# Operand stacks of a causal attention, built in another layout and filled through a scratch in memory

## The reference

```python
q = (x @ Wq.T).reshape(N, L, H, D).transpose(0, 2, 1, 3)     # H = 16 heads, D = 16
k = (x @ Wk.T).reshape(N, L, H, D).transpose(0, 2, 1, 3)
q = _layernorm(q, gq, bq)                                     # per head
k = _layernorm(k, gk, bk)
scores = jnp.einsum('nhld,nhmd->nhlm', q, k)
scores = jnp.where(causal, scores, NEG)
attn = jax.nn.softmax(scores, axis=-1)
```

## Time and profile before

| | us |
|---|---|
| median of 3 runs | 3621.69 (3620.69 to 3624.71) |
| the profiled execution | 3617.72 |
| its span, first to last instruction | 3615.8 |
| TensorE busy (matmuls) | 3336.7, 92% |
| VectorE busy | 2755.9, 76% |
| ScalarE busy | 2407.7, 67% |
| GpSimd busy | 1098.6, 30% |
| DMA queue of SP | 23.68 MB, 2.3% of 16 engines |

### The profile page before, as it was taken

How to read it: one execution, slowest core, us unless ns; L and a number is a source line. 1 busy time by engine, 2 the same in 40 slices (tenths; PEclk the granted TensorE clock), 3 DMA queues, 4 the chain that set the end, 5 groups by cost and what they waited for, 6 DMA issues and landing times.

```text
span 3615.8 us, 82601 instructions
## 1 busy us (share of the span) xinstructions
PE 3336.7 (92%) x31672; PEld 2617.6 (72%) x31672; DVE 2755.9 (76%) x5952; ACT 2407.7 (67%) x6425; POOL 1098.6 (30%) x778
## 2 busy tenths in 40 slices
PE   5999999999999999998999999999999999999998
PEld 4676776767777677776777767777676776767776
DVE  6877778777777877768777787787877878777775
ACT  6667676666766667666676666766667676666764
POOL 4351242412324223242222423124241242412320
PEclk8999999999999999999999999999999999999999
DMA  3000000000000000000000000000000000000000
GB/s 83 8 1 13 2 7 7 1 13 2 7 7 1 13 2 7 8 1 13 2 7 7 7 7 1 8 7 7 7 1 13 2 7 8 1 13 2 7 1 7
DMA packets 33863, 28.95 MB, mean 8 GB/s; under 512 B 8960, under 2 KB 33408, under 8 KB 33472
## 3 DMA queue, kind: packets, MB, share of 16 engines
q1 hardware_dynamic: 33472, 23.68, 2.3%
HBM read 15.28 MB, written 8.39 MB: 7 GB/s over the span
## 4 chain that ended last, share of the span: by engine, by line
PE 71%; ACT 14%; DVE 10%; issue 4%; POOL 1%; SPq 0%; DMA 0%; ACTq 0%; POOLq 0%; DVEq 0%
PE bank L696 14%; PE scores L810 11%; PE bank L707 9%; ACT prob L996 7%; PE scores L683 5%; PE bank L834 5%; PE scores L684 4%; PE scores L761 4%; PE scores L784 3%; PE bank L643 3%; PE scores L685 3%; PE bank L667 2%; DVE negmax L1265 2%; ACT qkt L937 2%; PE scores L679 2%
## 5 line engine op out<-in xcount | busy, mean ns | idle before, releaser
L996 ACT ACTIVATE prob<-scores,negmax 128x128 f32<-128x128 f32 (+3 forms) x2048 | 1059.3, 536 | 185.9 <-DVE negmax L1265 180.3
L1265 DVE TENSOR_REDUCE negmax<-scores 128x1 f32<-128x128 f32 (+3 forms) x2048 | 872.9, 482 | 54.8 <-PE scores L685 40.6
L696 PE MATMUL bank<-ident,prob 128*128 128x128 f32 x5120 | 725.8, 279 | 50.5 <-DVE probt L1273 43.4
L1273 DVE COPY probt<-bank 128x512 f32<-128x512 f32 x896 | 596.3, 683 | 171.5 <-PE bank L696 165.7
L696 PEld LDWEIGHTS bank<-ident,prob 128*128 128x128 f32 x5120 | 544.3, 141 | 163.7 <-issue 66.5
L685 PE MATMUL scores<-mask,ident 128*128 128x128 bf16 x2048 | 438.7, 226 | 0.0
L996 ACT ACTIVATION_READ_ACCUMULATOR prob<-scores,negmax 128x1 f32 x2048 | 434.8, 212 | 0.0
L683 PE MATMUL scores<-khh,qt 128*128 128x256 f32 (+2 forms) x1024 | 416.2, 407 | 13.3 <-POOL kll L572 13.3
L508 POOL TENSOR_TENSOR otl<-onm,oth 128x512 fp32r<-128x512 f32 x96 | 122.7, 1278 | 882.5 <-ACT oth L937 882.5
L521 POOL TENSOR_TENSOR rq<-ssq,expo 128x32 f32<-128x32 f32 x64 | 359.8, 5633 | 47.1 <-DVE ssq L1236 47.1
L503 POOL COPY rexp<-rsum 128x512 f32<-128x512 f32 x128 | 78.3, 611 | 964.8 <-DVE rsum L1277 964.8
(11 more groups left out here) (189 smaller groups left out, 6626.9 us busy)
## 6 DMA issues: line engine op xcount, KB each, us to landing
x_in<-in_x_rows SPq DMA_DIRECT2D x16, 512.0 KB, 3.8
out_rows<-x SPq DMA_DIRECT2D x16, 512.0 KB, 3.0
r_d<-in_wd SPq DMA_DIRECT2D x1, 1024.0 KB, 7.2
r_gu<-in_wg SPq DMA_DIRECT2D x2, 512.0 KB, 4.6
r_gu<-in_wu SPq DMA_DIRECT2D x2, 512.0 KB, 5.5
r_wob<-in_wo SPq DMA_DIRECT2D x4, 128.0 KB, 6.1
r_wqt<-in_wq_nope_t SPq DMA_DIRECT2D x1, 512.0 KB, 7.0
r_wqr<-in_wq SPq DMA_DIRECT2D x2, 256.0 KB, 8.5
```

Of the source, the lines that this page charges most:

```text
L696: ins = nc.tensor.transpose(bank[4 + n % 2][:, q * P:(q + 1) * P], prob[:, u % 2, q, i * P:(i + 1) * P], ident[:, :])
L996: nc.scalar.activation(prob[:, u % 2, q, 0:n], bank[q][:, 0:n], ACT.Exp, bias=negmax[:, a, u, q:q + 1], accum_out=sums[:, a, u, q:q + 1]). ...
L1265: nc.vector.tensor_reduce(negmax[:, a, u, M * part:M * part + M], scores[:, M * part:M * part + M, 0:n], axis=AX.X, op=ALU.max, negate=Tru ...
L1273: nc.vector.tensor_copy(probt[:, u % 2, i], bank[4 + n % 2][:, :]).then_inc(probt_dve.sem, 1)
```

## The change

The normalised queries and keys of a tile (512 channels, still fp32) are transposed first, in four fp32 transposes (`turn_qk`). Now channels are on partitions, in four blocks c, and tokens in rows. The split is made there: ScalarE copies the high part from PSUM and, later, the middle part (`high_part_qk`, `mid_part_qk`); VectorE makes the rest and the low part (`rest_qk`, `low_part_qk`). `part` holds the three parts of all four tiles. SP then stores each part to `stash` in memory (L459 of the new file) and loads it back into its slots of `qkt` (L466): a high part goes to three slots of the queries and three of the keys, a middle part to two and two, a low part to one and one. This is done for two halves, tokens 0 to 255 and 256 to 511: three stores and twelve loads each. A store has 128 partitions by 4 blocks by 256 tokens, a load 16 partitions (the channels of a head) by 16 heads by 256 tokens, so its rows have 512 bytes on both sides. Unit 0's scores wait for the first half's loads, unit 2's for the second half's; the first transposes of probabilities wait for all stores. The tables of steps are new.

```diff
-    res1 = at("res1", [P, 2 * C], F32, o + 10240)
-    stk = at("stk", [P, 2, 2 * H, SLOTS, D], BF16, o + 12288)
+    part = at("part", [P, 3, 4, L], BF16, o + 12288)
+    rest = at("rest", [P, 2, 4, P], F32, o + 24576)
...
+    stash = nc.dram_tensor("stash", (3, 4 * P, L), BF16, kind="Internal").ap()
...
-    QUADS_AT = {4: (0, 1, 2), 5: (3, 4, 5), 6: (6, 7), 7: (8, 9, 10), 8: (11, 12, 13), 9: (14, 15)}
-    CAST_AT = {2: 0, 3: 1, 5: 2, 6: 3}
-    REST_AT = {3: 0, 4: 1, 6: 2, 7: 3}
+    TURN_AT = {2: 0, 3: 1, 5: 2}
+    TURN_FIRST = {6: 3}
+    HIGH_AT = {3: (0,), 4: (1,), 6: (2, 3)}
+    MID_AT = {4: (0,), 5: (1,), 7: (2, 3)}
+    QUERY_SLOTS = ((0, 1, 2), (3, 4), (5,))
+    KEY_SLOTS = ((0, 3, 5), (1, 4), (2,))
...
+        def store_part(k, half, signal):
+            tokens = slice(half * 2 * P, (half + 1) * 2 * P)
+            sp.dma_start(stash[k].rearrange("(c p) l -> p c l", p=P)[:, :, tokens], part[:, k, :, tokens]).then_inc(signal.sem, 16)
+
+        def load_slots(k, half):
+            tokens = slice(half * 2 * P, (half + 1) * 2 * P)
+            for first, slots in ((0, QUERY_SLOTS[k]), (H, KEY_SLOTS[k])):
+                rows = stash[k][first * D:(first + H) * D].rearrange("(h d) l -> d h l", d=D)
+                for s in slots:
+                    sp.dma_start(qkt[s * D:(s + 1) * D, first:first + H, tokens], rows[:, :, tokens]).then_inc(stack_loaded[half].sem, 16)
+
+        def stack_rows(b, half):
+            if b > 0:
+                sp.wait_ge(stack_loaded[half].sem, stack_loaded[half].at(b, 0))
+            sp.wait_ge(high_ready.sem, high_ready.at(b, 2 * half + 2))
+            store_part(0, half, high_stored)
+            sp.wait_ge(mid_ready.sem, mid_ready.at(b, 2 * half + 2))
+            store_part(1, half, mid_stored)
+            sp.wait_ge(high_stored.sem, high_stored.at(b, 16 * (half + 1)))
+            load_slots(0, half)
+            sp.wait_ge(low_ready.sem, low_ready.at(b, 2 * half + 2))
+            store_part(2, half, low_stored)
+            sp.wait_ge(mid_stored.sem, mid_stored.at(b, 16 * (half + 1)))
+            load_slots(1, half)
+            sp.wait_ge(low_stored.sem, low_stored.at(b, 16 * (half + 1)))
+            load_slots(2, half)
...
+        for half in range(2):
+            stack_rows(0, half)
...
             sp.wait_ge(y_added.sem, y_added.at(b, NT))
             sp.dma_start(x_in[:, :, :], dram["x_rows"][bass.ds(b * L + L, L)].rearrange("(t p) c -> p t c", p=P)).then_inc(x_loaded.sem, 16)
+            for half in range(2):
+                stack_rows(b + 1, half)
             sp.wait_ge(down_added.sem, down_added.at(b, 1))
...
-        def transpose_quad(b, n):
-            t, quad = divmod(n, 4)
-            pe.wait_ge(stack_ready.sem, stack_ready.at(b, t + 1))
-            if n == 0:
+        def turn_qk(b, t):
+            pe.wait_ge(qhat_ready.sem, qhat_ready.at(b, t + 1))
+            if t == 0:
                 pe.wait_ge(sq_ready.sem, sq_ready.at(b, NT))
-            elif n == 1:
+            elif t == 1:
                 pe.wait_ge(v_ready.sem, v_ready.at(b, NT))
             else:
-                pe.wait_ge(stackt_act.sem, stackt_act.at(b, n - 1))
-            out = bank[6 + n % 2].bitcast(BF16)
-            for i in range(8):
-                ins = nc.tensor.transpose(out[:, i * P:(i + 1) * P],
-                                          stk[:, t % 2, quad * 8 + i].rearrange("p s d -> p (s d)"), ident16[:, :])
-            ins.then_inc(stackt_psum.sem, 1)
+                pe.wait_ge(rest_ready.sem, rest_ready.at(b, t - 1))
+            for c in range(4):
+                ins = nc.tensor.transpose(bank[6 + t % 2][:, c * P:(c + 1) * P], qn[:, t, c * P:(c + 1) * P], ident[:, :])
+            ins.then_inc(qkt_psum.sem, 1)
...
+            if a == 0 and part == 0 and u in (0, 2):
+                pe.wait_ge(stack_loaded[u // 2].sem, stack_loaded[u // 2].at(b, 2 * SPLITS * 16))
...
-                        pe.wait_ge(stackt_act.sem, stackt_act.at(b, 4 * NT))
+                        pe.wait_ge(rest_ready.sem, rest_ready.at(b, NT))
+                        pe.wait_ge(high_stored.sem, high_stored.at(b, 32))
+                        pe.wait_ge(mid_stored.sem, mid_stored.at(b, 32))
+                        pe.wait_ge(low_stored.sem, low_stored.at(b, 32))
...
-                    for n in QUADS_AT.get(e, ()):
-                        transpose_quad(b + 1, n)
+                    if e in TURN_FIRST:
+                        turn_qk(b + 1, TURN_FIRST[e])
                 if 1 <= e < NE:
                     spread_comb(b, e)
                 if e + 1 < NE:
                     gate_up(b, e + 1)
+                if e in TURN_AT and not last:
+                    turn_qk(b + 1, TURN_AT[e])
...
-        def cast_parts(b, t):
-            s = t % 2
-            act.wait_ge(qhat_ready.sem, qhat_ready.at(b, t + 1))
-            if t >= 2:
-                act.wait_ge(stackt_psum.sem, stackt_psum.at(b, 4 * (t - 1)))
-            qv = qn[:, t, 0:C].rearrange("p (h o d) -> p h o d", h=H, o=1)
-            kv = qn[:, t, C:2 * C].rearrange("p (h o d) -> p h o d", h=H, o=1)
-            copy(stk[:, s, 0:H, 0:3], qv.to_broadcast([P, H, 3, D]))
-            copy(stk[:, s, H:2 * H, 0:4:3], kv.to_broadcast([P, H, 2, D]))
-            copy(stk[:, s, H:2 * H, 5], kv[:, :, 0]).then_inc(part1_ready.sem, 1)
-
-        def copy_quad(b, n):
-            t, quad = divmod(n, 4)
-            act.wait_ge(stackt_psum.sem, stackt_psum.at(b, n + 1))
-            copy(qkt[:, quad * 8:(quad + 1) * 8, t * P:(t + 1) * P],
-                 bank[6 + n % 2].bitcast(BF16)[0:SD].rearrange("p (h t) -> p h t", h=8)).then_inc(stackt_act.sem, 1)
+        def high_part_qk(b, t):
+            act.wait_ge(qkt_psum.sem, qkt_psum.at(b, t + 1))
+            if b > 0 and t % 2 == 0:
+                act.wait_ge(high_stored.sem, high_stored.at(b - 1, 32))
+            copy(part[:, 0, :, t * P:(t + 1) * P], bank[6 + t % 2].rearrange("p (c l) -> p c l", c=4)).then_inc(high_ready.sem, 1)
+
+        def mid_part_qk(b, t):
+            act.wait_ge(rest_ready.sem, rest_ready.at(b, t + 1))
+            copy(part[:, 1, :, t * P:(t + 1) * P], rest[:, t % 2]).then_inc(mid_ready.sem, 1)
...
+            if a == 0 and u == 1 and part == 0:
+                act.wait_ge(mid_stored.sem, mid_stored.at(b, 32))
+                act.wait_ge(low_stored.sem, low_stored.at(b, 32))
...
-                    for n in QUADS_AT.get(e, ()):
-                        copy_quad(b + 1, n)
-                    if e in CAST_AT:
-                        cast_parts(b + 1, CAST_AT[e])
+                    for t in MID_AT.get(e, ()):
+                        mid_part_qk(b + 1, t)
+                    for t in HIGH_AT.get(e, ()):
+                        high_part_qk(b + 1, t)
...
-        def rest_parts(b, t):
-            s = t % 2
-            dve.wait_ge(part1_ready.sem, part1_ready.at(b, t + 1))
-            if t > 0:
-                dve.wait_ge(stack_ready.sem, stack_ready.at(b, t))
-            rv = res1[:, :].rearrange("p (h d) -> p h d", d=D)
-            chain.link(tt(rv, qn[:, t].rearrange("p (h d) -> p h d", d=D), stk[:, s, :, 0], ALU.subtract))
-            nc.vector.tensor_copy(stk[:, s, 0:H, 3:5], rv[:, 0:H].unsqueeze(2).to_broadcast([P, H, 2, D]))
-            chain.link(nc.vector.tensor_copy(stk[:, s, H:2 * H, 1:5:3], rv[:, H:2 * H].unsqueeze(2).to_broadcast([P, H, 2, D])))
-            tt(stk[:, s, 0:H, 5], rv[:, 0:H], stk[:, s, 0:H, 3], ALU.subtract)
-            tt(stk[:, s, H:2 * H, 2], rv[:, H:2 * H], stk[:, s, H:2 * H, 1], ALU.subtract).then_inc(stack_ready.sem, 1)
+        def rest_qk(b, t):
+            dve.wait_ge(high_ready.sem, high_ready.at(b, t + 1))
+            if t >= 2:
+                dve.wait_ge(low_ready.sem, low_ready.at(b, t - 1))
+            tt(rest[:, t % 2], bank[6 + t % 2].rearrange("p (c l) -> p c l", c=4), part[:, 0, :, t * P:(t + 1) * P],
+               ALU.subtract).then_inc(rest_ready.sem, 1)
+
+        def low_part_qk(b, t):
+            dve.wait_ge(mid_ready.sem, mid_ready.at(b, t + 1))
+            tt(part[:, 2, :, t * P:(t + 1) * P], rest[:, t % 2], part[:, 1, :, t * P:(t + 1) * P], ALU.subtract).then_inc(low_ready.sem, 1)
...
+                    for t in MID_AT.get(e, ()):
+                        low_part_qk(b + 1, t)
                     if e == 3:
                         scale_qk(b + 1, 2)
-                    if e in REST_AT:
-                        rest_parts(b + 1, REST_AT[e])
+                    for t in HIGH_AT.get(e, ()):
+                        rest_qk(b + 1, t)
                     if e == 4:
```

More of the change, by code:

```diff
@@ L42 @@
 SPLITS = 6
-SLOTS = 8
 SD = SPLITS * D
@@ L276, in _build @@
     padded = sem("padded")
-    part1_ready = Signal(sem("part1_ready"), NT)
-    stack_ready = Signal(sem("stack_ready"), NT)
-    stackt_psum = Signal(sem("stackt_psum"), 4 * NT)
-    stackt_act = Signal(sem("stackt_act"), 4 * NT)
+    qkt_psum = Signal(sem("qkt_psum"), NT)
+    high_ready = Signal(sem("high_ready"), NT)
```

(40 more changed lines are left out.)

16 lines of the change are left out of this document (9 added, 7 removed).

## The result

The changed kernel takes 3696.32 us (median of 4 runs, 3692.46 to 3698.74) where the kernel before took 3621.85 beside it (4 runs, 3620.69 to 3624.71). The ratio is 1.0203, with a 95% interval of 1.0186 to 1.0221: it is slower by 2%, and the kernel before varies by 0.1%. The profiled execution took 3694.8 us, its span 3693.0, at a mean granted clock of 0.965 (before: 0.995).

A forecast was written before the change was run, and what follows sets the result against it. The chain of waits lay on TensorE for 71% of the span. From 3617.7 us, +63 for 15 batch changes and +8.9 for the first batch gave 3690, shown as a median of 3694, 4 higher; range 3550 to 3770.

The forecast's parts named there:

- What goes: TensorE, ScalarE and VectorE at each batch change: old stack transposes, evictions and subtractions leave, gaining 7.7 us a batch.
- the tail: TensorE from the last gate and up product to expert 8's down product: 5.6 us instead of 7.18, saving 1.6.
- The additions on ScalarE and VectorE are hidden: Expert steps: at most 1.3 us of ScalarE copies and 1.9 of VectorE subtractions fit under 4.38 us, costed at nothing.
- A load takes 1.1 us: DMA queue: each 128 KB load into 16 partitions takes 1.1 us, estimated from the r_oa loads.
- The queue's schedule: SP's stores and loads: second half lands at 520.8 us, where TensorE would reach unit 2 at 508.9; 11.9 lost.
- Nothing for the colder TensorE: TensorE after its two waits: half clock costed at nothing, though 1 us a batch would be +15.
- The first batch: Program start, no experts to hide under: transfers end at 80.5 us, where unit 2's scores started at 71.62; +8.9.
- +4.2 a batch: Each batch change: 7.7 us gained by the engines, 11.9 lost to transfers; times 15 is +63.
- A: DMA queue: neighbouring loads overlap, only SP's issue counts, nobody waits; 3507 us; chance 0.28 with its middle cases.
- B: DMA queue: each load takes 1.28 us, both halves late, +8.5 a batch; 3762 us; chance 0.21 with beyond.
- C: DMA queue: loads take 0.90 to 0.95 us, waits return what transposes gave; 3620 to 3636 us; chance 0.06.

## Why the prediction was right

The forecast was 3694, measured 3696.3. Its steps, one by one:

- **What goes** held. Steps with a turn take 4.81 to 4.83 us and those without 4.37 (predicted 4.78 and 4.38), the tail 5.60 (predicted 5.6). Without transfers the distance to unit 2 shrank by 7.43 us in the batch shown and by 6.98 in the mean, predicted 7.7, and a batch by 7.08.
- **The additions on ScalarE and VectorE are hidden**: held, since the steps show nothing of them.
- **A load takes 1.1 us**, chosen between 0.43 and 1.28: measured 1.03 to 1.12 (127 to 117 GB/s). The r_oa loads in one window of before carried this number, and the runs with 32 and 128 partitions show that it was read for the right reason. The Trainium skill's "SBUF — State Buffer", section "Door 1: The DMA port swizzle", gives 104 GB/s for partitions 0 to 15 and 189 for 0 to 31. Measured here are 111 to 127 and 180 to 200, so by the page's figures the loads would come out slower than they are (it led to 3756). Its order of the two holds. Its table has no row for 48 partitions, but its map of ports gives 0 to 15 and 32 to 47 the same four ports, which could be why the loads into 0 to 47 moved only 140; no run here shows whether it is.
- **The queue's schedule** held nearly everywhere: unit 0 does not wait; the first transposes run at 525.00 - 11.61 = 513.4 (predicted 513.9); unit 2's scores at 519.4 (predicted 520.8). So at unit 2 the batch is behind by 2.8 us, in the mean of 13 batches by 167.39 - 164.13 = 3.3, where 4.2 was predicted.
- **Nothing for the colder TensorE**: this step failed. Behind the waits the clock is at its lower level, and keeping TensorE busy gives back 1.65 us a batch and 26 us in all. The text named 1 us a batch as a possibility and left it out, on the ground of a sparse start that showed little of it. There no batch followed to measure by; here unit 4 comes 7.84 us after unit 2 where it was 7.08.
- **The first batch** was put at 8.9 us and took 7.05 by its next x_in issue. That is 10.6 us of transfers less 3.5 us that the engines save there (137.33, 126.75 without transfers, 130.28 before). The prediction gave the engines nothing in the first batch.

So +4.2 a batch came out as 4.55, but in the mean from -7.0 (predicted -7.7), +10.2 at unit 2 (predicted +11.9) and +1.3 of what follows (predicted 0). The transfers were over-rated by 1.7 us a batch, the gain by 0.7, and what the waits cost behind unit 2 was left out. That the total agrees within 3 us is in part this cancelling, and so luck: 1.7 us a batch alone would have moved it by some 25 us, 1.3 by 20. The sum in the profiled frame: 7.05 for the first batch, 14 x 4.55 = 63.7 up to the last x_in issue, and 6.5 behind it make 77.2, which is 3693.0 - 3615.8, where 63 + 8.9 = 71.9 was predicted.

**The rivals.** A, the transfers fit, did not happen, but its price was right: 3510.8 without transfers and 3515 to 3519 with transfers that fit, against 3507. The point from which it decides, 0.93 us a load, held only for the schedule as written. With the loads cut by heads the same slow loads fit. B and C did not happen: the loads were neither at 1.28 us nor at 0.90.

**Open**: why loads into 48 partitions are slower than those into 32; and whether, in the changed kernel, two narrow loads on different queues would overlap. That wasn't tried.

## What to carry to other kernels

Read a transfer's rate from rows that hit as few partitions as yours will, not from the kernel's big loads: here the same row size and bytes meant 127 GB/s into 16 partitions and 200 into 32. Where a queue is late, first ask which of its bytes the waiting instruction reads. Sending those ahead, and the stores that it waits for, was worth 3696 - 3515 = 181 us here without any faster transfer, where the layout that raised the rate from 127 to about 218 GB/s gave back 40. And when TensorE is to stand idle for several microseconds, price the clock behind the wait as a term of its own.

## What the runs showed of the hardware

- A full share says nothing of the rate: at 1.15 to 1.28 it went with 113, 127, 140, 196, 216 and 341 GB/s.
- Stores in pieces of 64 KB took SP 0.57 us each at least and moved 90 to 143 GB/s with the engines at 0.34 to 0.63 of their share, where whole ones of 256 KB took it 0.45 and moved 250 to 280. With all of them issued they still moved no more than 170, at 0.57.
- SP's issue of six loads takes 2.7 to 3.1 us with room in the queue, and 6.4 to 7.0 behind others. What stands after it in SP's order, a store that is ready included, waits as well (8 us for the low parts above).
- TensorE stood still from 518.9; its clock was at the lower level from 524 to 534, through the rest of the first wait, the second and the first 3 us of work behind it. With TensorE kept busy a batch took 1.65 us less, although ScalarE and VectorE share that chain.
